# Summing the direct half over d once per four units: a running sum on VectorE in place of three of four small matmuls

## The reference

```python
for i in range(3):
    z = jnp.einsum('bmd,bnd->bmnd', x, hidden).reshape(B, -1, D)
    cur = jnp.einsum('bcd,co->bod', z, Ws[i]) + bs[i][None, :, None]
    cur = jax.nn.relu(cur)
    if i != 2: hidden, direct = (cur[:, :100, :], cur[:, 100:, :])
    else:      direct = cur
    finals.append(direct)
return jnp.sum(jnp.concatenate(finals, axis=1), axis=-1)      # sum over d: (512, 400)
```

## Time and profile before

| | |
|---|---|
| median of three runs | 2921.08 us (2919.97 to 2921.81) |
| the profiled execution: its own time | 2919.57 us |
| its span in the profile | 2917.8 us |
| busy: TensorE, VectorE, ScalarE | 97%, 91%, 64% |
| mean share of the 16 DMA engines | 43.9% |

### The profile page before, as it was taken

How to read it: one execution, slowest core, us unless ns; L and a number is a source line. 1 busy time by engine, 2 the same in 40 slices (tenths; PEclk the granted TensorE clock), 3 DMA queues, 4 the chain that set the end, 5 groups by cost and what they waited for, 6 DMA issues and landing times.

```text
span 2917.8 us, 58694 instructions
## 1 busy us (share of the span) xinstructions
PE 2820.6 (97%) x18688; PEld 2666.4 (91%) x18688; DVE 2668.5 (91%) x2706; ACT 1873.7 (64%) x3850; POOL 1.1 (0%) x11
## 2 busy tenths in 40 slices
PE   1699999999999999999999999999999999999998
PEld 1699999999999999999999999999999999999998
DVE  3799999999999999999999999999999999999997
ACT  2466666666666666666666666666666666666665
POOL 0000000000000000000000000000000000000000
PEclk8899999999999999999999999999999999999999
DMA  8344444344444344344344344344444434444441
GB/s 193 84 130 107 107 128 110 106 127 113 104 125 117 104 124 118 104 120 121 104 118 124 104 117 125 104 112 129 104 109 128 108 107 127 111 106 126 113 106 53
DMA packets 256151, 333.83 MB, mean 114 GB/s; under 512 B 61346, under 2 KB 190990, under 8 KB 256014
## 3 DMA queue, kind: packets, MB, share of 16 engines
q1 hardware_dynamic: 256138, 333.67, 43.9%
HBM read 332.73 MB, written 8.37 MB: 117 GB/s over the span
## 4 chain that ended last, share of the span: by engine, by line
PE 95%; DMA 2%; DVE 1%; SPq 1%; ACT 1%; issue 0%; DVEq 0%; ACTq 0%
PE acc L589 62%; PE acc L590 28%; PE summed L608 4%; PE turned L601 1%; DMA xb<-x_by_unit 0%; DMA xb<-in_L_rec_b_dram 0%; DVE z_low L346 0%; DMA w_rows_again<-in_L_rec_W_dram 0%; DMA xb<-in_L_rec_W_dram 0%; DVE z L342 0%; DVE w_split L319 0%; DMA out_dram<-o_row 0%; ACT w_split L487 0%; ACT z_high L454 0%; SPq L194 0%
## 5 line engine op out<-in xcount | busy, mean ns | idle before, releaser
L589 PE MATMUL acc<-w_split,z_high 128*128 128x400 f32 (+1 forms) x8832 | 2672.9, 368 | 77.5 <-DVE z_low L346 71.6
L590 PE MATMUL acc<-w_split,z_low 128*128 128x200 f32 (+1 forms) x8832 | 2255.7, 255 | 0.0
L589 PEld LDWEIGHTS acc<-w_split,z_high 128*128 128x128 f32 (+1 forms) x8832 | 1661.5, 188 | 166.9 <-issue 159.3
L454 ACT ACTIVATE z_high<-z 128x1024 fp32r<-128x1024 f32 (+2 forms) x1152 | 1179.3, 1024 | 814.9 <-PE acc L590 737.5
L590 PEld LDWEIGHTS acc<-w_split,z_low 128*128 128x128 f32 (+1 forms) x8832 | 1690.9, 191 | 0.0
L346 DVE TENSOR_TENSOR z_low<-z,z_high 128x1024 fp32r<-128x1024 f32 (+2 forms) x1152 | 1353.4, 1175 | 129.3 <-ACT z_high L454 129.2
L342 DVE TENSOR_TENSOR z<-hid,xb 128x1024 f32<-128x1024 f32 (+1 forms) x1024 | 1213.8, 1185 | 59.7 <-DMA xb<-x_by_unit 50.9
L475 ACT ACTIVATE hid<-turned 96x512 f32<-96x512 f32 x256 | 149.1, 582 | 132.2 <-PE turned L601 132.2
L478 ACT ACTIVATE hid<-turned 32x128 f32<-32x128 f32 x768 | 204.6, 266 | 8.9
L608 PE MATMUL summed<-s,group_b 128*4 128x100 f32 (+1 forms) x768 | 150.1, 277 | 1.4 <-ACT s L470 1.4
L351 DVE TENSOR_TENSOR s<-acc,half 128x200 f32<-128x200 f32 x384 | 137.8, 359 | 10.5 <-ACT half L459 10.5
(11 more groups left out here) (20 smaller groups left out, 13.5 us busy)
## 6 DMA issues: line engine op xcount, KB each, us to landing
xb<-x_by_unit SPq DMA_DIRECT2D x384, 384.0 KB, 4.8
x_right<-x_by_unit SPq DMA_DIRECT2D x384, 136.5 KB
xb<-x_by_unit SPq DMA_DIRECT2D x384, 128.0 KB, 5.7
xb<-x_by_unit SPq DMA_DIRECT2D x128, 336.0 KB
xb<-x_by_unit SPq DMA_DIRECT2D x128, 84.0 KB
x_left<-x_by_unit SPq DMA_DIRECT2D x384, 19.5 KB
out_dram<-o_row SPq DMA_DIRECT2D x256, 1.6 KB
xb<-in_L_rec_W_dram SPq DMA_DIRECT2D x6, 600.0 KB, 9.2
```

Source lines behind the costliest of these rows:

```text
L454: nc.scalar.activation(z_high[slot][0:rows, 0:n * T], z[slot][0:rows, 0:n * T], ACT.Copy).then_inc(high, 1)
L589: nc.tensor.matmul(a[:, 0:2 * O], z_high[slot][0:rows, tok], w, start=(c == 0), stop=False, skip_group_check=True)
L590: last = nc.tensor.matmul(a[:, 0:O], z_low[slot][0:rows, tok], w[:, 0:O], start=False, stop=(c == chunks - 1), skip_group_check=True)
```

## The change

A unit now holds 8 values of d (`STEPS`) of 16 rows (`BT`), and four units in a row (q = 0 to 3 of `QUARTERS`) hold the 32 values of d of the same 16 rows. The direct half is no longer summed over d by TensorE in each unit: VectorE applies the relu and keeps a running sum `direct[l]` over the four units (`directs`), and TensorE sums that one over the 8 partitions of a row once per four units. `relu` on ScalarE is gone; `results` and `send` come once per four units. `turn_x` copies runs of 8 values (32 bytes) where it copied runs of 32 (128 bytes). The loops hold four periods.

```diff
-BT = T // D
+QUARTERS = 4
+STEPS = D // QUARTERS
+BT = T // STEPS
...
-            def turn_x(u):
+            def turn_x(rows, q):
...
-                src = [[D, F], [F * D, BT], [1, D]]
-                dst = [[T, F], [D, BT], [1, D]]
...
+                src = [[D, F], [F * D, BT], [1, STEPS]]
+                dst = [[T, F], [STEPS, BT], [1, STEPS]]
...
             def sums(l, u):
                 dve.wait_ge(half_in[l], u + 1)
+                if not (isinstance(u, int) and u == 0):
+                    dve.wait_ge(direct_in[l], u)
...
+            def directs(l, rows, q):
+
+                u = rows * QUARTERS + q
+                part = s[l][:, 1, 0:HID] if l < 2 else s[l][:, :, :].rearrange("p h o -> p (h o)")
+                dve.wait_ge(s_in[l], u + 1)
+                if q == 0:
+                    if not (isinstance(rows, int) and rows == 0):
+                        dve.wait_ge(direct_summed[l], rows)
+                    nc.vector.tensor_scalar(direct[l][:, :], part, 0.0, None, ALU.max).then_inc(direct_in[l], 1)
+                else:
+                    dve.wait_ge(direct_in[l], u)
+                    nc.vector.scalar_tensor_tensor(direct[l][:, :], part, 0.0, direct[l][:, :], ALU.max, ALU.add).then_inc(direct_in[l], 1)
...
-            def relu(l, u):
-                act.wait_ge(s_in[l], u + 1)
-                part = s[l][:, 1, 0:HID] if l < 2 else s[l][:, :, :]
-                nc.scalar.activation(part, part, ACT.Relu).then_inc(relu_done[l], 1)
...
-            def sum_over_d(l, u):
-                pe.wait_ge(relu_done[l], u + 1)
...
+            def sum_over_d(l, rows):
+                pe.wait_ge(direct_in[l], rows * QUARTERS + QUARTERS)
...
-                sum_over_d(1, n - 1)
+                if j == 0:
+                    sum_over_d(1, m - 1)
                 multiply(1, base + 1, slot(1), 1)
-                if before0:
-                    sum_over_d(0, n + 1)
+                if j == 2:
+                    sum_over_d(0, m)
...
-                    sum_over_d(2, n - 2)
...
+                if before2 and j == 1:
+                    sum_over_d(2, m - 1)
```

More of the change, by code:

```diff
@@ L96, in cin_kernel @@
         group_b = sb("group_b", [P, BT])
+        direct = {l: sb(f"direct{l}", [P, DIRECT[l]]) for l in range(3)}
         o_row = {l: sb(f"o_row{l}", [BT, DIRECT[l]]) for l in range(3)}
@@ L258, in period @@
                 if turn:
[L259 to L262, removed]
+                    turn_x(m + 1, j)
+                if j == 0:
+                    send(1, m - 1)
+                if j == 2 and layer0:
+                    send(0, m)
                 if pairs:
@@ L269, in period @@
                         load_xb(n + 1, 1 - par, g)
[L270 to L274, removed]
+                if j == 1 and not (isinstance(m, int) and m == 0):
+                    send(2, m - 1)
             sp.wait_ge(xt_done, 160)
@@ L277, in _ @@
             load_pairs(3)
[L278 to L288, removed]
+            for j in range(1, QUARTERS):
+                period(0, j)
+            with sp.Fori(0, UNITS // QUARTERS - 2) as i:
+                for j in range(QUARTERS):
+                    period(i + 1, j)
+            last = UNITS // QUARTERS - 1
+            period(last, 0, turn=False)
+            period(last, 1, pairs=False, turn=False)
+            period(last, 2, layer0=False, pairs=False, turn=False)
+            period(last, 3, layer0=False, pairs=False, turn=False, ahead=False)
+            send(0, last)
+            send(1, last)
+            send(2, last)
             for l in range(3):
-                sp.wait_ge(o_out[l], 16 * (UNITS + 1))
+                sp.wait_ge(o_out[l], 16 * (UNITS // QUARTERS + 1))
         @block.gpsimd
@@ L428, in period @@
                 lows(base + q + 2, slot(q + 2), P, group_chunks(2))
+                directs(1, m, j)
                 if layer0:
                     sums(0, n + 2)
[L432 to L437, removed]
+            period(0, 1, first(1), first(1) % RING, before2=False, last_low=False)
+            period(0, 2, first(2), first(2) % RING)
+            period(0, 3, first(3), first(3) % RING)
+            with dve.Fori(0, UNITS // QUARTERS - 2) as i:
+                for j in range(QUARTERS):
+                    period(i + 1, j, first(i * QUARTERS + (QUARTERS + j)), first(j + QUARTERS) % RING)
+            last = UNITS // QUARTERS - 1
+            for j in range(QUARTERS):
+                n = last * QUARTERS + j
+                period(last, j, first(n), first(n) % RING, layer0=j < 2, before0=j < 3)
             at = first(UNITS)
@@ L507, in _ @@
                     dup(0, 1)
-                    relu(0, 1)
                 if k == 7:
                     hidden(0, 1, 1)
-                    results(0, 1)
             at = first(0)
@@ L570, in _ @@
                 highs(at + g, slot_of(at + g), P, group_chunks(g))
-            results(1, UNITS - 1)
-            relu(2, UNITS - 2)
-            results(2, UNITS - 2)
+            results(1, last)
             second_half(2, UNITS - 1, at + 3)
-            relu(2, UNITS - 1)
-            results(2, UNITS - 1)
+            results(2, last)
         @block.tensor
@@ L601, in transpose @@
                 nc.tensor.transpose(turned[l][:, 0:T], s[l][:, 0, :], ident[:, :]).then_inc(turned_in[l], 1)
[L603 to L608 removed]
+            def sum_over_d(l, rows):
+                pe.wait_ge(direct_in[l], rows * QUARTERS + QUARTERS)
+                if not (isinstance(rows, int) and rows == 0):
+                    pe.wait_ge(o_in[l], rows)
+                nc.tensor.matmul(summed[l][0:BT, 0:DIRECT[l]], group_b[:, :], direct[l][:, :], start=True, stop=True,
                                  skip_group_check=True).then_inc(direct_summed[l], 1)
```

121 lines of the change are left out of this document (66 added, 55 removed).

## The result

The changed kernel takes 2800.34 us (median of four runs, 2798.15 to 2802.31) against 2921.07: ratio 0.9587, 95% interval 0.9570 to 0.9603. The forecast was 2815, the range 2799 to 2872. The time lies at its lower edge; the way there is mostly the one foretold, and one term was missing. One of the executions behind the experiments, of e_room, ran at a mean granted clock of 0.66 and took 3722 us; its ratio leaves that one out.

A forecast was written before the change was run, and what follows sets the result against it. TensorE bounds the kernel, VectorE close behind; the change moves the bound to VectorE. 126 periods x (21.95 - 21.10) = 107 us; 2919.57 less 107 plus 1 is 2813.5, forecast 2815 us given the median offset, range 2799 to 2872.

The forecast's parts named there:

- The range: Whole kernel: 8 in 10 for 2799 to 2872 us, leaving out the lower rival, kept wait and slow pieces.
- The likeliest case: VectorE becomes the bound: 2815 us, 2807 to 2848 by the bounds of the new instructions; chance 0.65.
- TensorE's loss: TensorE's sums over d fall from 1.52 to 0.38 us per unit, taking its period from 21.95 to 20.81 us.
- VectorE's work: VectorE's 20.48 us of work per period plus 0.62 for three directs gives 21.10, between 21.04 and 21.36.
- The high bound: VectorE's three directs overlap nothing and each takes its full record: 0.88 us per unit.
- The bound moves: From TensorE (20.81 us) to VectorE (21.10), losing some 0.3 us of TensorE's saving; rival that TensorE stays: 0.10.
- The wait of 0.79 us: VectorE's wait for z_high ahead of z_low goes, with 0.5 us of room; rival: stays partly 0.11, wholly 0.04.
- xb: VectorE's waits for xb loads behind send(0): up to 0.7 us in one of four periods, taken as 0.
- turn_x: 944 pieces of 32 bytes per unit, at most 4.7 us, hidden; rival that they hold up the loads: 0.05.
- The longer loop: Rival, chance 0.05: TensorE's doubled loop is fetched again at each of 31 turns, +45 us, 2860 us.
- Start and end: Two small VectorE instructions and two larger turn_x ahead of the weight copies add 1 us, a guess.
- What would show it: Signs: VectorE over 98% busy, TensorE near 98.6% with idle time before L620, 0.79 us wait gone, xb waits under 20.

The follow-up runs named there:

- e_room: Kernel before the change, with three added instructions on VectorE where the change has its directs, on constant tiles, TensorE's sums kept: 2920.72 us, ratio 1.0000.
- e_first: Changed kernel keeping only the first of each four running sums on VectorE, so the sum is incomplete: 2770.29 us, ratio 0.9484.
- e_double: Changed kernel with one more instruction of the same kind and size behind each directs on VectorE, into an unread scratch tile: 2870.97 us, ratio 0.9829.
- e_after_late: Changed kernel with send(0) moved behind the loads of pairs and xb in SyncE's list: 2795.66 us, ratio 0.9570.
- e_wide: Changed kernel with turn_x copying runs of 128 bytes again, so sums run over other values than the reference's: 2798.81 us, ratio 0.9583.
- e_act0: Changed kernel with the first of each four running sums done by ScalarE instead of VectorE: 2800.80 us, ratio 0.9590.

## Why the prediction was right, point by point

- **The range.** That the time fell inside it is partly luck. The likeliest case was worked out as 2807 to 2848, and 2800.34 lies below that. The foot of the range, 2799, has no working in the prediction, and the time cleared it by 1.3 us.
- **TensorE's loss.** Forecast 20.81 us per period; e_first has 20.86, of which at most 20.83 are TensorE's by the medians. The sums cost 0.44 and 0.60 us or a little more there, forecast 0.45 and 0.62. Right.
- **VectorE's work.** Forecast 21.10 us, measured period 21.088. Adding up the median distance of each place in the four periods, about 21.02 of it are work and 0.07 waits. The new instructions cost what `sums` had told, 0.17 and 0.27 us, and the first of four 0.12 and 0.17: 0.57 us per unit, where the sum took 0.62. The work of before was 20.45 rather than 20.48. So the period came out within 0.01 because two small errors met: 0.08 us too much work, and 0.07 us of waits put at nothing. The high bound, 0.88 us per unit with each instruction at its full record, is ruled out by a row of three (e_double).
- **The bound moves.** Right: e_double pays for nearly all that is added to VectorE (0.57 of 0.61 us), e_room for none of it, e_first gets back 0.22. The prediction compared two means, though, and the four periods are not alike: VectorE's work is 20.92, 21.07, 21.02 and 21.07 us in them, and TensorE's, by e_first, 20.90, at most 20.46, 20.91 and 21.06. In two of them the two engines are within 0.02 us of each other.
- **The wait of 0.79 us.** Right that it goes. In one period of four 0.14 is left of it (1559.90 to 1561.05 in the last section is 1.15 us, not 1.00). It comes after layer 2's sum, which delays the transpose by 0.6 us, more than the room of 0.5 that I had worked out. That is how it looks in the distances; no run moved that sum.
- **xb.** I put up to 0.17 us on the mean in the range and 0 in the sum. It was 0.034, 4.7 us in all (e_after_late).
- **turn_x.** Hidden, as forecast (e_wide). 90624 packets more on q1 raised the engines' time from 0.439 x 16 x 2917.8 to 0.477 x 16 x 2798.1, by 870 us: 0.01 us a packet, about an eighth of my high bound of 0.08. The Trainium skill, DMA: Bandwidth & Descriptors, section Specifications, has a read-modify-write for pieces under 512 bytes. No run shows whether it took place; e_wide shows that pieces of 32 instead of 128 bytes cost this kernel no time.
- **The longer loop.** 13 packets on q8 instead of 7, for a loop of twice the length and 30 turns (the prediction has 31): no fetch per turn.
- **Start and end: the term that was mis-sized.** I wrote +1 us, a guess from one issue time. The three steady periods at the end that my 126 took in gave 2.8, as they should. The start gave -9.1. The error of 14.7 us in the median is 10.1 from this term (1 + 9.1) and 3.6 from the periods (107.8 + 2.8 instead of 107); the last 1.0 is that the profiled execution before lay 1.5 us under its median and the one after 0.5. I had looked at windows for the first 100 us and read the low clock and the weight loads there, but not the waits by name, where "DMA out_dram<-o_row 12.4" stood on ScalarE's `results`, an instruction that the change thins out.
- **What would show it.** I wrote that TensorE would be busy near 98.6% with idle time ahead of L620. It shows 99.9%. The test was a bad one: TensorE's busy time is the same in e_first, which it bounds, and falls where VectorE is further behind (98.8% in e_double).

## What to carry to other kernels

When work is moved from the bounding engine to one at 94%, work out the new period as the larger of two sums of distances from start to start, and do it for each kind of period if they differ; a gain of 1.14 us on one engine was 0.88 on the clock, since the other had no room for more. Look in the start and the tail for each instruction that the change removes or thins out, and read what it waits for: a wait there is paid once, but it was 8% of this gain. A change on the new bounding engine that "does nothing" (e_act0) may have met the next wait; try that wait before giving the change up, and expect that it brings less than it takes off (0.04 of 0.10 us here).

## What the runs showed of the hardware

- In the changed kernel VectorE's records stretch over a run of instructions without a wait, and the distance between starts does not (timeline of VectorE, around the 0.14 us wait):

```profile
1558.76 1.26 DVE L354 TENSOR_TENSOR z_low<-z,z_high 128x1024 fp32r<-128x1024 f32 x1
1559.90 1.13 DVE L350 TENSOR_TENSOR z<-hid,xb 128x896 f32<-128x896 f32 x1
1561.05 1.23 DVE L354 TENSOR_TENSOR z_low<-z,z_high 128x1024 fp32r<-128x1024 f32 x1
```

  The same z_low goes from 1.22 up to 1.26 us and falls back once VectorE has waited (1559.90 to 1561.05 is 1.15, not 1.00). A duration that has risen by up to 3% (1.4% on the mean, 1220 to 1237 ns) is not slower work here; distances between starts are what to add up. It is no sure sign of a saturated engine either: in e_double, busy for 2399.75 of 2400 us, the mean is 1220 ns.
- Adding `s` to the running sum on GpSimd, beside a busy VectorE, took 4.2 us on the mean and up to 6.6 for 128x200, and 2.7 and up to 9.1 for 128x100, where VectorE took 0.27 and 0.17 from start to start.
